# Attention scores on four 32x32 parts of TensorE, ScalarE writing q tiles and the mask, and split buffers of their own for x and ctx

## What is computed

```python
def xattn(x, cond, Wq, bq, Wk, bk, Wv, bv, Wo, bo):   # HEADS = 8, WINDOW = 16, hd = 16
    q = pointwise(Wq, bq, x); k = pointwise(Wk, bk, cond); v = pointwise(Wv, bv, cond)
    k = pad(k, 8, 7); v = pad(v, 8, 7)
    k_win = k[:, :, idx]; v_win = v[:, :, idx]         # idx[t, w] = t + w
    dots = einsum('bhdt,bhdtw->bhtw', q, k_win) * hd ** -0.5
    out = einsum('bhtw,bhdtw->bhdt', softmax(dots), v_win)
    return pointwise(Wo, bo, out)

def ffn(x, gate_w, lora_A, lora_B):                    # 8 experts, top 2, rank 64
    weights, sel = top_k(softmax(x @ gate_w.T), 2); weights /= sum(weights)
    return sum over e of w_full[:, e] * (x @ lora_A[e].T @ lora_B[e].T)

x = x + xattn(layernorm(x), ctx, ...)
x = x + ffn(layernorm(x), ...)
```

## Time and profile before

| | before |
|---|---|
| time, median of 3 runs | 1185.83 us (1184.03 to 1186.89) |
| the profiled execution | 1181.87 us |
| its span on the core | 1180.1 us |
| TensorE busy | 1118.5 us, 95% |
| weight loads busy | 965.0 us, 82% |
| VectorE busy | 904.6 us, 77% |
| GpSimd busy | 408.9 us, 35% |
| ScalarE busy | 391.8 us, 33% |
| granted TensorE clock, mean | 0.99 |

### The profile page before, as it was taken

One profiled execution on the slowest core, in us unless ns is written; L12 is line 12 of the kernel. 1 busy time (PEld: TensorE's weight loads), 2 busy tenths in 40 slices (PEclk: granted clock), 3 DMA queues, 4 the chain that ended last, 5 costly groups with the idle time before them and its releaser, 6 DMA issues.

```text
span 1180.1 us, 38884 instructions
## 1 busy us (share of the span) xinstructions
PE 1118.5 (95%) x16384; PEld 965.0 (82%) x16384; DVE 904.6 (77%) x2021; ACT 391.8 (33%) x553; POOL 408.9 (35%) x302
## 2 busy tenths in 40 slices
PE   1677999999999999999999999999999999999987
PEld 1566888888888888888888888888888888888875
DVE  3576787877778787787878787888778787877763
ACT  3323433333333333333332333323333333233221
POOL 4443333333323334333333433333343233333210
PEclk9988999999999999999999999999999999999999
DMA  7344334455443355443345543434554433454200
GB/s 226 68 90 90 93 86 79 91 109 104 89 96 81 72 108 109 94 96 93 77 81 110 109 89 95 94 70 92 110 108 90 95 86 75 97 110 91 56 37 36
DMA packets 423345, 108.68 MB, mean 92 GB/s; under 512 B 405904, under 2 KB 406032, under 8 KB 423056
## 3 DMA queue, kind: packets, MB, share of 16 engines
q1 hardware_dynamic: 423184, 106.11, 41.6%
HBM read 55.22 MB, written 16.78 MB: 61 GB/s over the span
## 4 chain that ended last, share of the span: by engine, by line
PE 83%; DVE 4%; issue 4%; POOL 4%; SPq 3%; ACT 1%; DMA 1%; DVEq 0%; POOLq 0%; ACTq 0%
PE bank_a L314 29%; PE bank_b L342 19%; PE bank_c L314 15%; PE bank_b L363 14%; PE bank_a L372 4%; PE bank_b L332 2%; SPq L240 2%; DMA raw<-x 1%; DVE stats L616 1%; POOL prob L842 1%; SPq L249 1%; POOL attn_split L863 1%; POOL src_split L857 1%; POOL src_split L848 1%; ACT k_sb L591 1%
## 5 line engine op out<-in xcount | busy, mean ns | idle before, releaser
L342 PEld LDWEIGHTS bank_b<-k_sb,q_diag 64*64 64x64 f32 x8192 | 249.8, 135 | 29.6 <-issue 29.6
L342 PE MATMUL bank_b<-k_sb,q_diag 64*64 64x32 f32 x8192 | 264.0, 220 | 0.0
L842 POOL TENSOR_TENSOR prob<-prob,row_inv 128x512 f32<-128x512 f32 x128 | 134.2, 1048 | 262.1 <-DVE row_inv L705 262.1
L314 PE MATMUL bank_a<-down_split,mid_split 128*128 128x264 f32 (+1 forms) x1536 | 216.8, 291 | 1.8 <-DVE mid_split L748 1.8
L363 PEld LDWEIGHTS bank_b<-prob_t,v_diag 64*64 64x64 f32 x4608 | 187.6, 133 | 25.8 <-issue 16.4
L314 PE MATMUL bank_c<-src_split,w_split 128*128 128x512 f32 x576 | 161.9, 418 | 49.0 <-ACT k_sb L591 22.8
L363 PE MATMUL bank_b<-prob_t,v_diag 64*64 64x96 f32 (+2 forms) x4608 | 201.7, 238 | 0.9 <-DMA v_diag<-v_t 0.9
L314 PEld LDWEIGHTS bank_a<-down_split,mid_split 128*128 128x128 f32 x1536 | 191.4, 188 | 7.1 <-ACT mid_split L545 1.9
L314 PE MATMUL bank_a<-up_split,ht_split 128*128 128x512 f32 x768 | 188.7, 395 | 1.5 <-DVE ht_split L787 1.5
L528 ACT ACTIVATE prob<-prob 128x512 f32<-128x512 f32 x128 | 80.8, 631 | 296.5 <-DVE prob L693 294.7
L314 PEld LDWEIGHTS bank_c<-src_split,w_split 128*128 128x128 f32 x576 | 107.5, 196 | 81.0 <-ACT k_sb L591 32.4
(11 more groups left out here) (68 smaller groups left out, 1100.8 us busy)
## 6 DMA issues: line engine op xcount, KB each, us to landing
v_diag<-v_t SPq DMA_DIRECT2D x128, 132.0 KB, 5.4
raw<-x SPq DMA_DIRECT2D x32, 512.0 KB, 4.4
raw<-ctx SPq DMA_DIRECT2D x32, 512.0 KB, 5.8
q_diag<-q_xn SPq DMA_DIRECT2D x256, 64.0 KB, 3.6
resid_pair<-x SPq DMA_DIRECT2D x32, 512.0 KB, 3.2
out<-resid_pair SPq DMA_DIRECT2D x32, 512.0 KB, 2.6
v_diag<-up_w SPq DMA_DIRECT2D x1, 2048.0 KB, 10.6
prob_t<-down_w SPq DMA_DIRECT2D x1, 780.0 KB, 6.2
```

The costliest lines, as they stand in the source:

```text
L314: return nc.tensor.matmul(dst, st[:, s, st_cols], mv[:, m, mv_cols], start=start and n == 0, stop=stop and n == 2)
L342: last = nc.tensor.matmul(bank_b[m % 2][rows, t * KT:(t + 1) * KT], q_diag[rows, cur.parity, n, :], keys[rows, n * QT:n * QT + KT], start= ...
L842: nc.gpsimd.tensor_tensor(weights_of(m), weights_of(m), row_inv[:, cols].unsqueeze(2).broadcast_to([P, CT, KT]), ALU.mult).then_inc(prob_d ...
```

## The change

- **Scores**: the stationary of a tile is 32 rows by 32 columns (2 heads x 16 queries), in four parts on the diagonal of the array, not 64 by 64 in two. `q_diag` shrinks to 32 columns a tile.
- **q tiles**: ScalarE writes `q_diag` itself, with two activations straight from PSUM whose scale and bias are zero on the heads that don't belong; the eight DMAs and `q_xn2`'s part in it go (`xn2` remains for the second norm).
- **Mask**: TensorE's mask matmul goes, except for two at the very start. After each chunk's exponentials ScalarE copies the mask into the bank, where the next chunk but one is added to it.
- **High copies**: ScalarE writes the high parts of ctx, attn and xn (xn by a second activation); VectorE's three copies go.
- **Buffers**: `src_split` becomes `x_split` and `ctx_split`; the ctx load moves to the end of `later`'s step, so it is a step ahead.
- **Order**: score chunk 0 of `ahead` is computed inside `up`; k is projected before score chunk 3; the waits that open a chunk are moved ahead of the last pass before it. All engines' orders are rewritten to match.
- **Weights**: six pieces in place of five; GpSimd splits four of them (low parts), VectorE two.

```diff
@@ tensor
-            def open_scores(cur, m):
-                if m >= 2 or cur.c >= 1:
-                    pe.wait_ge(shifted, cur.count(CHUNKS, m - 1))
-                nc.tensor.matmul(bank_b[m % 2][:], mask_rows[:], mask_cols[:],
-                                 start=True, stop=False, skip_group_check=True)
+            def open_scores(b, m):
+                if m == 0:
+                    pe.wait_ge(k_out, b.count(1, 1))
+                    pe.wait_ge(q_out, b.count(2, 2))
+                if m >= 2 or b.c >= 1:
+                    pe.wait_ge(mask_set, b.count(CHUNKS, m - 1))
...
-                    for z in range(HALVES):
-                        rows = slice(z * HALF_P, (z + 1) * HALF_P)
+                    for g in range(PAIRS):
+                        rows = slice(PW * g, PW * (g + 1))
...
                     for e in range(EK):
+                        if e == EK - 1 and ahead:
+                            open_scores(ahead, 0)
                         up(0, e)
...
+                    scores_chunk(ahead, 0)
@@ scalar
             def exponentials(cur, m):
                 act.wait_ge(shifted, cur.count(CHUNKS, m + 1))
                 nc.scalar.activation(weights_of(m), weights_of(m), ACT.Exp).then_inc(exp_done, 1)
+                nc.scalar.activation(bank_b[m % 2][:], mask[:], ACT.Copy).then_inc(mask_set, 1)
+
+            def place_q(ahead):
+                act.wait_ge(q_done, ahead.count(1, 1))
...
+                for h in range(2):
+                    nc.scalar.activation(q_diag[:, ahead.parity, :, h * QT:(h + 1) * QT],
+                                         bank_c[:].rearrange("p (n i) -> p n i", i=QT), ACT.Identity,
+                                         bias=bq_scaled[:, h:h + 1],
+                                         scale=consts[:, 4 + h:5 + h]).then_inc(q_out, 1)
...
+                    act.wait_ge(ctx_in, ahead.count(16, 16))
+                    nc.scalar.activation(ctx_split[:, 0, :], ctx_of(ahead), ACT.Copy).then_inc(ctx_hi, 1)
...
+                    for target in (x_split[:, 0, :], raw[:]):
+                        last = nc.scalar.activation(target, raw[:], ACT.Identity, bias=shift[:, 0:1],
+                                                    scale=rstd[:, 0:1])
@@ sync
-                if ahead:
-                    sp.wait_ge(xn_lo, ahead.count(1, 1))
-                    sp.dma_start(raw[:], ctx[ahead_row]).then_inc(raw_in, 16)
...
-                    place_q(ahead)
                 if later:
                     if later.c >= 1:
+                        sp.wait_ge(xn_lo, later.count(1, 0))
+                    if later.c >= 2:
                         sp.wait_ge(ctx_lo, later.count(1, 0))
-                    sp.dma_start(raw[:], x[later_row]).then_inc(raw_in, 16)
+                    sp.dma_start(raw[:], x[later_row]).then_inc(x_in, 16)
...
+                        sp.wait_ge(xn_lo, later.count(1, 1))
+                        sp.dma_start(raw[:], ctx[later_row]).then_inc(ctx_in, 16)
@@ vector, the new order of a step
+                if cur:
+                    weights_transpose(cur, 0)
+                    v_transpose(cur)
+                if old:
...
+                if prev:
+                    join_heads(prev, 2)
+                if cur:
+                    scores_shift(cur, 1)
+                    weights_sum(cur, 1)
+                    weights_transpose(cur, 1)
+                if prev:
+                    join_heads(prev, 3)
+                if later:
+                    first_norm()
+                    first_shift()
+                if old:
+                    choose_experts(old)
...
+                    weigh_experts(old, 0)
+                if cur:
+                    scores_shift(cur, 2)
+                if old:
+                    weigh_experts(old, 1)
+                if cur:
+                    weights_sum(cur, 2)
+                    join_heads(cur, 0)
+                    weights_transpose(cur, 2)
...
+                if cur:
+                    scores_shift(cur, 3)
+                    if prev:
+                        residual()
+                    weights_sum(cur, 3)
+                    if prev:
+                        second_norm()
+                    join_heads(cur, 1)
+                    if prev:
+                        second_shift()
...
+                    scores_shift(ahead, 0)
...
+                    weights_sum(ahead, 0)
@@ gpsimd, the new order of a step
+                    weights_norm(cur, 0)
+                if ahead and ahead.c >= 1:
+                    context_lo(ahead)
                 if cur:
                     weights_norm(cur, 1)
...
```

More of the change, by code:

```diff
@@ L306, in _ @@
         def _(pe):
+            pe.wait_ge(small_in, 16 * 4)
+            for m in range(2):
+                nc.tensor.matmul(bank_b[m][:], ident[:], mask[:], start=True, stop=False, skip_group_check=True)
             pe.wait_ge(weights_lo, 1)
-            pe.wait_ge(masks_ready, 2)
             pe.wait_ge(pads_zero, 7)
@@ L444, in step @@
                     for f in range(4, FK):
+                        if f == FK - 1 and cur:
+                            open_scores(cur, 2)
                         down(0, f)
-                score(2)
+                if cur:
+                    if not old:
+                        open_scores(cur, 2)
+                    scores_chunk(cur, 2)
+                if prev and not cur:
+                    project_o()
                 if old:
@@ L458, in step @@
                         down(1, f)
-                score(3)
+                if cur:
+                    if ahead:
+                        project_k()
+                    else:
+                        open_scores(cur, 3)
+                    scores_chunk(cur, 3)
                 if old:
```

456 lines of the change are left out of this document (229 added, 227 removed).

## The result

The kernel after takes **1265.54 us** (median of 4 runs, 1263.59 to 1273.51), the kernel before 1185.12 beside it: ratio **1.069** (95% interval 1.064 to 1.074), slower by 6.9%. The forecast was 1128 us (range 1078 to 1175). The profiled execution spans 1261.8 us. One of run 3's four executions and one of run 5's ten were over 1.5% above their fastest; medians take these slow ones in, ratios leave them out.

A forecast was written before the change was run, and what follows sets the result against it. TensorE sets the pace before the change, VectorE's path of work and waits after it. Start 85, 29 batches of 33.3 and tail 73 give 1124 us, 1126 with 1.8 outside the span, 1128 as median; range 1078 to 1175.

The forecast's parts named there:

- Four parts run at once: TensorE's scores: four parts of the array work simultaneously, so a chunk takes 1.14 us instead of 1.99.
- The rival with a least distance between instructions: TensorE's score matmuls keep a minimum spacing, making the kernel slower; 1381 us at today's 31 ns; chance 0.13.
- the rival on ScalarE's writes: Mask copy into PSUM costs far more or its order stalls TensorE: 1145 to 1175 us; chance 0.04.
- The pauses between sum and transpose: VectorE waits for GpSimd's norm before transposing prob, three times a batch: 1.25, 1.25 and 0.85 us, 3.3 together.
- those for exponentials: VectorE waits for exp before its sums: 0.8 us for chunk 1, 0.5 for chunk 2, 1.3 a batch.
- x's: VectorE waits for the load of x before the first norm: 1.3 us a batch.
- TensorE's for k_sb: TensorE's output projection waits for ScalarE's late evacuation of k: 0.7 to 1.5 us of TensorE's slack.
- The two signs that were to make the prediction wrong: A score chunk over 2.4 us, or x landing over 12 us after v_t's start.
- 26.4 us a batch: VectorE's busy work without the three high copies, 25.7 us, plus 0.7 for small hand-overs.
- the 33.3 us: VectorE's path per batch: 26.4 us of work plus waits of 3.3, 1.3, 1.0 and 1.3.
- I take 0, since by the next part TensorE has 3 us to spare in a batch: Loop branch on TensorE's sequencer: some 0.6 us may show, 13 times, 8 us if TensorE bound; priced at zero.
- Some 3 us of idle time a batch: TensorE's slack, mostly before down's first part (for mid's low half) and before o (for k).

The follow-up runs named there:

- run 3: Kernel after with both edits: GpSimd waits for the first norm's shift, and filler matmuls where TensorE waits for h_sb and k_sb; 1234.29 us, ratio 1.037.
- run 5: Kernel after with GpSimd's low half of attn ahead of the power of the first norm instead of behind it; 1178.75 us, ratio 0.994.
- run 1: Kernel after with GpSimd starting attn's low half only once VectorE has finished the first norm's shift; 1249.66 us, ratio 1.057.
- run 18: run 13's kernel with x's load behind two v placements (1117.86 us), and GpSimd's power ahead of attn's low half again; 1158.69 us, ratio 0.977.
- run 4: Kernel before with only the scores changed, to four 32x32 parts; 1285.10 us, ratio 1.088.
- run 11: Kernel before with all steps written out, no loop, nothing else changed; 1182.39 us, ratio 0.997.
- run 6: Kernel after with all 34 steps written out and no loop; 1210.19 us, ratio 1.021.
- run 17: run 13's kernel with x's load behind two v placements (1117.86 us), and the loop put back; 1131.73 us, ratio 0.956.
- run 8: Kernel after with attn's low half ahead of the power on GpSimd, and all steps written out without a loop; 1151.08 us, ratio 0.972.
- run 7: Kernel before with the scores on four parts and all steps written out without a loop; 1205.73 us, ratio 1.017.
- run 2: Kernel after with 9 unused filler matmuls where TensorE waits for h_sb and 3 where it waits for k_sb; 1244.27 us, ratio 1.049.
- run 13: run 8's kernel with heads joined between the second chunk's shift and sum, and the first norm's shift behind the third expert-choosing step; 1122.98 us, ratio 0.949.
- run 16: run 13's kernel with x's load behind two v placements (1117.86 us), and k_sb written ahead of the third chunk's exponential; 1150.30 us, ratio 0.972.
- run 12: run 7's kernel with each score chunk in four pieces of 32 matmuls between slower passes; 1256.98 us, ratio 1.061.

## Why the prediction was wrong

**What held.** Four parts run at once: 1.22 us a chunk against 1.14 forecast, instead of 1.99. The rival with a least distance between instructions is out: 128 matmuls in 1.22 us are 9.5 ns each. The Trainium skill's rule of about 25 ns (TensorE: Matmul & The Clock Gate, "Wait — 56ns, not 53.3ns?") doesn't hold for tiles of 32 rows on four row groups; Part 3 of that page, by which their starts can be 4 ns apart, is not contradicted. The mask copy takes 0.58 us (0.6 forecast), the two q writes 2.29, so the rival on ScalarE's writes is out too; ScalarE is busy 46%. The pauses between sum and transpose are 1.16, 1.17 and 0.85 us (1.25, 1.25, 0.85), those for exponentials 0.7 and 0.37 (0.8, 0.5), x's 1.66 (1.3), TensorE's for k_sb 1.29 (0.7 to 1.5). Tail 74.7 (73), start 92 (85). The two signs that were to make the prediction wrong hardly came: three of 128 chunks took over 2.4 us, none of them between 200 and 1000 us, and VectorE's statistics of x began 10.1 us after v_t's start in the median, once 12.2.

**The first step that failed is VectorE's own work, "26.4 us a batch"**, the largest term of the 33.3 us. It took each operation at its length of before, where GpSimd's subtractions lay elsewhere. In the new order the power and attn's low half follow each other on GpSimd, so that the shift, which waits for the power, met the subtraction in 29 of 32 batches: + 2.2 us a batch. The trace of before could have told: attn's cast took 1197 ns in the mean and ctx's, the same size, 698, and I called both their plain lengths. In fact 24 of the 32 attn casts took 1.33 us, and they began while GpSimd was scaling prob; the six that overlapped with that by 0.13 us at most took 0.69, ctx's length. One of the long ones, VectorE's row and then GpSimd's:

```profile
634.31 1.33 DVE L770 CAST attn_split<-attn 128x1024 fp32r<-128x1024 f32 x1
...
634.04 1.05 POOL L842 TENSOR_TENSOR prob<-prob,row_inv 128x512 f32<-128x512 f32 x1 [0.69 <-DVE row_inv L705]
```

The Trainium skill, SBUF — State Buffer, "Who interferes with whom", states it: a VectorE operation with two inputs in SBUF, or in a two-port mode, and a GpSimd one that reads SBUF exclude each other for a whole instruction. The shift (two inputs) and the cast of run 1 agree with it, 2.35 and 1.98 us for 0.16 and 0.17; I had not put it among the rivals. Runs 5 and 18 price the order at 87 and 41 us.

**The second is "I take 0, since by the next part TensorE has 3 us to spare in a batch"**, said of the branch, and with it that TensorE's slack costs nothing. Two things were missing there.
- *Instructions have to arrive.* I asked at what rate the engine can start matmuls, not at what rate it is given them. The change makes 1528 loads and matmuls of 1024 a batch; they come in packets of 16 KB, in run 4 over 3 us apart, and 256 of them go in 1.25 us. Behind a branch they come late: in after two packets start at 739.1 and 739.8, just behind the branch at 738.8, and v starts at 743.7, 1.8 us after the second has landed. The branch is covered in the kernel before (run 11: 3 us), costs 55 us in after (run 6), and 14 to 28 where less else is late (runs 17, 8). The Trainium skill, Runtime: NRT & Kernel Launch, "Instruction fetch mechanics", has the 16 KiB blocks of 256 instructions and the stall at a taken branch, and the traces agree with both (216 packets for 55268 instructions, 4.2 to 4.9 us at a taken branch of after); that crossing a block is "mostly hidden" is wrong here, with 90 us of gaps in run 4. Between 200 and 1000 us run 8 has 22 us of it, run 7 56 (where part are steps of 0.16 us ahead of each chunk). Run 8's chunks start 7.3 us apart at the least, run 7's 5.6; that the spacing makes the difference is my reading, no run changes it alone.
- *Behind idle stretches the clock was halved.* Some 3 us of idle time a batch were forecast, with a stop before o for k_sb, but priced at nothing; the other stop was forecast before down's first part, for mid's low half. None came there; it stood before the transposes of h, for h_sb. Behind these stops the clock is 0.50, and two groups take 5.6 us instead of 3.1. With the stops filled (run 2) it wasn't, which gave 21 us in this kernel.

**What was right after all is the path itself.** With the held operation and the branch out of the way (run 8) a batch takes 33.81 us from one v_t to the next on average, beside the 33.3 of the sum and the 37.58 of after; the total is 1151 where 1128 was forecast. Term by term, VectorE's waits a batch in run 8 (its sums from 200 to 1000 us over 23.7 batches) are 3.2 us before the transposes of prob (forecast 3.3), 1.1 for exponentials (1.3), 1.7 for the two shifts (1.0) and 1.0 for x (1.3). Of the 3.8 us between, the runs give 3.0 to the order on GpSimd (34.56 in run 5) and 2.0 to the branch (35.63 in run 6), which overlap by 1.2. That VectorE's path sets the pace there is shown by run 13, where 1 us less of its waits a batch is 28 us of the total, and run 16 agrees, with 1 us more and 32. The 23 us that run 8 lies above the forecast (26 in its profiled execution) are 6 of start and, from v projection to v projection (33.98 us), 0.7 us a batch; the missing instructions of one chunk in four, 0.9 us a batch, would account for these, but no run shows that they do.

**Not settled**: what in a branch makes the difference between 4.3 us (after) and 3.4 (before). The traces differ in this: in after, two packets start 0.1 to 1.3 us apart behind each of its 12 taken branches, while in before and in run 4 no two start less than 3.0 us apart. Nor is it settled why run 17 loses only 14 us by the loop and run 6's kernel 55, with nearly the same gaps ahead of v (17.4 and 17.6 us from 200 to 1000); or what keeps packets 3 us apart in run 4, since behind a branch they can come closer.

## What to carry to other kernels

When work is moved from VectorE to GpSimd or in time, lay the two timelines beside each other: each small VectorE operation of a kind that was held here (a cast, a scalar_tensor_tensor on SBUF) that would fall beside a long GpSimd one is to be priced at the long one's rest, and exchanging two neighbours on GpSimd can be worth more than the whole change. Count instructions, too: splitting a matmul into more, smaller ones is only as good as the rate at which they arrive, so look at what stands just ahead of each dense group, keep each in one piece (run 12), and write a loop out once to see what its branch costs. And don't price TensorE's slack at nothing: behind stops of 2.7 and 1.3 us the next groups took 2.6 us more, at half clock, of which filling the stops gave back 0.7 us a batch (run 2).

## What the runs showed of the hardware

- A VectorE operation of one or two columns takes 0.16 us, and 2.0 to 2.35 us when GpSimd is subtracting 1024 columns; scalar_tensor_tensor and cast on SBUF were held, bn_stats, maximum, index search, a tensor_scalar on one column, transposes and operations with an input from PSUM were not. In the kernel before, a cast of 1024 columns took 1.33 us instead of 0.69 beside GpSimd's scaling of 512.
- 32x32 float32 matmuls on four row groups: 128 with their weight loads in 1.22 us, 9.5 ns each, while instructions last. Instructions arrive 256 at a time, in run 4 in packets 3.1 us apart at the least and 4.5 in the median, but 0.1 to 1.3 us apart behind branches of after; a TensorE that ran out of them inside a chunk resumed 1.2 to 1.7 us after a packet had landed (runs 4, 7 and 8).
- A taken branch holds TensorE's sequencer 4.2 to 4.9 us in after, 3.3 to 3.9 in before.
- A change from 128x128 to 32x32 tiles cost about 0.17 us and one back 0.07 (run 12).
- Behind stops of 2.7 and 1.3 us TensorE's granted clock was 0.50 for 5.65 us.
